# One piece split in each of eight epochs from the first sample on, with the second half's pieces first

## What is computed

```python
pooled = jnp.mean(x, axis=(2, 3))              # x is the normalized input here
att = jax.nn.sigmoid(pooled @ att_w.T + att_b)
agg_w = jnp.einsum('nk,kocij->nocij', att, weight)
out = conv_general_dilated(xi[None], wi, (1, 1), padding=[(1, 1), (1, 1)])   # per sample
x = x + conv(gn(x), weight, att_w, att_b)
```

## Time and profile before

| | |
|---|---|
| median of 3 runs | 1337.74 us (1337.7 to 1338.12) |
| the profiled execution | 1337.87 us |
| its span in the profile | 1335.7 us |
| TensorE (PE) busy | 1287.5 us, 96% |
| VectorE (DVE) busy | 1209.1 us, 91% |
| ScalarE (ACT) busy | 916.6 us, 69% |
| group matmuls, L480 | 6912, 1160.2 us |
| fp32 mix matmuls, L433 | 440, 74.7 us |
| fp16 mix matmuls, L442 | 1140, 87.1 us |

### The profile page before, as it was taken

How to read it: one execution, slowest core, us unless ns; L and a number is a source line. 1 busy time by engine, 2 the same in 40 slices (tenths; PEclk the granted TensorE clock), 3 DMA queues, 4 the chain that set the end, 5 groups by cost and what they waited for, 6 DMA issues and landing times.

```text
span 1335.7 us, 22954 instructions
## 1 busy us (share of the span) xinstructions
PE 1287.5 (96%) x8596; PEld 731.8 (55%) x8596; DVE 1209.1 (91%) x2121; ACT 916.6 (69%) x1441; POOL 56.8 (4%) x72
## 2 busy tenths in 40 slices
PE   1899999999999999999999999999999999999998
PEld 0455555555555555555555555555555555555555
DVE  7988999999999999999999998999989999998983
ACT  4875767867667676676867767677776767667531
POOL 0000000000000000000000000000000000000000
PEclk9899999999999999999999999999999999999999
DMA  9214644446543555534455452555525255552434
GB/s 381 99 22 125 180 115 104 129 130 176 143 107 108 137 157 145 144 89 133 141 145 156 98 145 77 149 139 145 145 54 153 84 146 145 128 154 60 98 98 142
DMA packets 30475, 174.59 MB, mean 131 GB/s; under 512 B 3488, under 2 KB 3744, under 8 KB 28320
## 3 DMA queue, kind: packets, MB, share of 16 engines
q1 hardware_dynamic: 20288, 113.94, 23.1%
q0 software_dynamic: 8928, 49.78, 22.2%
q10 hardware_dynamic: 1152, 9.44, 2.2%
HBM read 112.33 MB, written 51.38 MB: 123 GB/s over the span
## 4 chain that ended last, share of the span: by engine, by line
PE 95%; issue 4%; DVE 1%; POOL 0%; POOLq 0%; DVEq 0%
PE pM L480 86%; PE pG L442 4%; PE pG L433 4%; PE pS L415 0%; DVE Us L655 0%; DVE E L642 0%; POOL small L1321 0%; DVE Vs L660 0%; DVE T L636 0%; POOL sel L1317 0%; DVE X L767 0%; DVE small L901 0%; DVE small L890 0%; DVE small L889 0%; DVE small L891 0%
## 5 line engine op out<-in xcount | busy, mean ns | idle before, releaser
L480 PE MATMUL pM<-Vs,Us 128*128 128x385 f16 (+1 forms) x6912 | 1160.2, 330 | 2.6 <-DVE Us L655 2.6
L480 PEld LDWEIGHTS pM<-Vs,Us 128*128 128x128 f16 x6912 | 673.5, 98 | 495.7 <-issue 23.2
L1026 ACT CAST Vs<-E 128x784 f16<-128x784 f32 x192 | 159.8, 840 | 137.3 <-DVE E L628 72.2
L603 DVE SCALAR_TENSOR_TENSOR T<-X 128x392 f32<-128x392 f32 x384 | 193.4, 560 | 12.2 <-ACT X L1081 10.5
L660 DVE TENSOR_TENSOR Vs<-E,Vs 128x784 f16<-128x784 f32 x192 | 182.9, 969 | 4.0 <-ACT Vs L1026 4.0
L628 DVE SCALAR_TENSOR_TENSOR E<-T 128x784 f32<-128x784 f32 x128 | 119.1, 972 | 2.2
L1041 ACT ACTIVATE Us<-E 128x768 f16<-128x768 f32 x120 | 95.9, 835 | 35.6 <-DVE E L642 35.6
L642 DVE SCALAR_TENSOR_TENSOR E<-G,T 128x768 f32<-128x768 f32 x128 | 117.0, 955 | 2.2
L1101 ACT ACTIVATE unused<-X,small 128x784 bf16<-128x784 f32 x120 | 113.8, 949 | 3.9
L1062 ACT ACTIVATE X<-pM,small 128x392 f32<-128x392 f32 x128 | 74.6, 583 | 59.3 <-PE pM L480 59.2
L655 DVE SCALAR_TENSOR_TENSOR Us<-E,Us 128x768 f16<-128x768 f32 x120 | 111.8, 952 | 0.1
(11 more groups left out here) (83 smaller groups left out, 646.9 us busy)
## 6 DMA issues: line engine op xcount, KB each, us to landing
X<-x_dram SPq DMA_DIRECT2D x66, 784.0 KB, 5.4
out_dram<-X SPq DMA_DIRECT2D x64, 784.0 KB, 3.8
X<-x_dram POOLq DMA_DIRECT2D x62, 784.0 KB, 8.1
W<-w_dram SPq DMA_DIRECT2D x8, 1152.0 KB, 19.7
G<-W ACTq DMA_DIRECT2D x8, 1152.0 KB, 5.6
attw<-attw_dram SPq DMA_DIRECT2D x1, 128.0 KB, 8.3
small<-attb_dram SPq DMA_DIRECT2D x1, 0.5 KB, 8.9
```

The lines of the kernel that those rows point to most:

```text
L480: mm = pe.matmul(tile_rows(bank(k, o))[:, :, first:last], Us[:, j, a, c, o, kx, :], v_in(j, b, c, kx), start=(at < 2 and i == 0), stop=(i ...
L603: ins = dve.scalar_tensor_tensor(out=dst[c], in0=a[c], scalar=scale, in1=d[c], op0=ALU.mult, op1=ALU.add)
L1026: act.copy(v_out(j, 0), e_buf(n, ("V", chunk, j))).then_inc(v_hi, 1)
```

## The change

`SPLIT` now splits pieces 4, 5, 6, 7, 0, 1, 2, 3 in epochs 0 to 7, where epochs 1 to 8 split 0, 4, 1, 5, 2, 6, 3, 7. The mix waits for low parts in `mix_tile`, at tile 0 if a new piece is of half 0 and at tile 4 for all. In `epoch`, `w_low` comes before `v_low(n, 1, 4)`, `attention` and `add_rows(n, b, 3, 1)`. In the first epoch TensorE has logits and mix units earlier, and the lists of VectorE and ScalarE and their tables are in another order, with the split of piece 4 in them.

```diff
-SPLIT = ((), (0,), (4,), (1,), (5,), (2,), (6,), (3,), (7,))
+SPLIT = ((4,), (5,), (6,), (7,), (0,), (1,), (2,), (3,))
...
 U_LO_FIRST = [
-    (0, 2), (0, 1), (1, 2), (1, 1), (0, 3), (1, 3), (0, 0), (0, 4),
-    (1, 0), (1, 4), (1, 5), (0, 5),
+    (0, 1), (0, 2), (1, 1), (1, 2), (0, 3), (1, 3), (1, 0), (1, 4),
+    (0, 0), (0, 5), (0, 4), (1, 5),
 ]
...
             def mix_tile(n, m):
                 if not is_first(n) or m >= MIX_BANKS:
                     pe.wait_ge(taps_taken, n * TAKES + m - MIX_BANKS + 1)
+                if not is_first(n) and m in (0, FULL):
+
+                    new = [i for i in split_in(n - 1) if m == FULL or i < JT]
+                    if new:
+                        pe.wait_ge(w_lo, len(split_before(n - 1)) + len(new))
...
                 if u == 0:
                     pe.wait_ge(att_ready, n + 1)
-                    if split_in(n - 1):
-                        pe.wait_ge(w_lo, len(split_before(n)))
...
             group(0, 5, 0)
+            logits_mm(1)
             group(0, 5, 1)
             group(0, 6, 0)
-            logits_mm(1)
             group(0, 6, 1)
+            mix(1, 0)
             group(0, 7, 0)
             group(0, 7, 1)
             group(0, 8, 0)
-            mix(1, 0)
+            mix(1, 1)
             group(0, 8, 1)
-            mix(1, 1)
...
                 v_low(n, 1, 0)
                 add_rows(n, b, 3, 0)
+                if len(split_in(n)) > 0:
+                    w_low(n, 0)
                 v_low(n, 1, 4)
                 if more:
                     attention(n + 1)
                 add_rows(n, b, 3, 1)
-                if len(split_in(n)) > 0:
-                    w_low(n, 0)
```

More of the change, by code:

```diff
@@ L78 @@
 V_LO_FIRST = [
[L79 to L80 removed]
+    (0, 3), (0, 4), (0, 0), (0, 1), (0, 2), (1, 1), (0, 5), (1, 2),
+    (1, 0), (1, 3), (1, 5), (1, 4),
 ]
@@ L922, in _ @@
             norm_too(0, 0, 1, 1)
+            w_max(1)
             norm_too(0, 0, 1, 0)
-            v_pair(0, 0, 0, 3)
             dve.wait_ge(pool_step, K + 1)
             attention(0)
-            v_pair(0, 0, 0, 1)
+            w_max(0)
+            v_pair(0, 0, 0, 3)
+            v_single(0, 0, 0, 0)
             v_low(0, 0, 3)
             v_low(0, 0, 4)
-            w_max(1)
-            v_single(0, 0, 0, 5)
-            w_max(0)
+            v_pair(0, 0, 0, 1)
+            v_low(0, 0, 0)
+            u_pair(0, 0, 1)
             v_low(0, 0, 1)
-            u_pair(0, 0, 1)
             w_bound()
@@ L937, in _ @@
             w_scale()
-            v_low(0, 0, 5)
             unscales()
             u_pair(0, 1, 1)
+            u_low(0, 0, 1)
             u_low(0, 0, 2)
-            u_low(0, 0, 1)
+            u_low(0, 1, 1)
             u_low(0, 1, 2)
-            u_low(0, 1, 1)
             u_pair(0, 0, 3)
@@ L948, in _ @@
             u_low(0, 1, 3)
-            v_single(0, 0, 0, 0)
+            u_low(0, 1, 0)
+            v_single(0, 0, 0, 5)
+            u_low(0, 1, 4)
             u_low(0, 0, 0)
+            u_low(0, 0, 5)
             u_low(0, 0, 4)
             v_pair(0, 0, 1, 1)
-            v_low(0, 0, 0)
-            u_low(0, 1, 0)
+            v_single(0, 0, 1, 5)
+            v_low(0, 1, 1)
+            u_low(0, 1, 5)
             take_other(0, 2, 0)
-            u_low(0, 1, 4)
-            u_low(0, 1, 5)
-            u_low(0, 0, 5)
+            channel_stats(1)
+            take_other(0, 3, 0)
+            group_shift(1)
+            take_other(0, 2, 1)
+            group_variance(1)
+            take_edge(0, 0, 4, 0)
+            v_low(0, 0, 5)
+            norm_scale(1)
+            take_other(0, 3, 1)
+            take_edge(0, 0, 4, 1)
             v_pair(0, 0, 1, 3)
-            v_low(0, 1, 1)
-            take_other(0, 3, 0)
-            take_other(0, 2, 1)
+            v_low(0, 1, 2)
             v_single(0, 0, 1, 0)
[L964 to L970, removed]
+            w_low(0, 0)
+            attention(1)
+            v_low(0, 1, 0)
+            take_edge(0, 0, 5, 0)
             v_low(0, 1, 3)
-            take_edge(0, 0, 4, 1)
-            norm_scale(1)
-            take_edge(0, 0, 5, 0)
             take_edge(0, 0, 5, 1)
             add_rows(0, 0, 3, 0)
+            add_rows(0, 0, 3, 1)
             v_low(0, 1, 5)
             v_low(0, 1, 4)
-            attention(1)
-            v_low(0, 1, 0)
-            add_rows(0, 0, 3, 1)
             v_pair(1, 1, 0, 1)
             v_pair(1, 1, 0, 3)
+            take_other(0, 8, 0)
             v_low(1, 0, 1)
@@ L986, in _ @@
             v_low(1, 0, 2)
-            take_other(0, 8, 0)
             u_pair(1, 0, 1)
             take_other(0, 9, 0)
+            add_rows(0, 0, 9, 0)
+            take_other(0, 8, 1)
+            take_other(0, 9, 1)
+            v_low(1, 0, 4)
             u_low(1, 0, 1)
-            add_rows(0, 0, 9, 0)
-            v_low(1, 0, 4)
-            take_other(0, 8, 1)
+            u_pair(1, 1, 1)
+            take_edge(0, 0, 10, 0)
             u_low(1, 0, 2)
-            u_pair(1, 1, 1)
             u_pair(1, 1, 3)
-            take_other(0, 9, 1)
             u_low(1, 1, 1)
-            take_edge(0, 0, 10, 0)
             take_edge(0, 0, 10, 1)
@@ L1235, in _ @@
             take_taps(0, 8)
-            u_high(0, 0, 0)
+            sums(1, 1, 0, 0)
             u_high(0, 0, 1)
             u_high(0, 0, 2)
-            u_high(0, 0, 5)
+            u_high(0, 1, 1)
             u_high(0, 1, 2)
-            u_high(0, 1, 1)
+            sums(1, 1, 0, 1)
             u_high(0, 1, 0)
-            sums(1, 1, 0, 0)
+            u_high(0, 0, 0)
             u_high(0, 0, 3)
             u_high(0, 1, 3)
-            u_high(0, 0, 4)
[L1247 to L1251, removed]
+            u_high(0, 0, 5)
+            sums(1, 1, 1, 0)
+            u_high(0, 1, 4)
+            take_first(0, 0, 1)
+            take_first(0, 0, 0)
+            u_high(0, 0, 4)
+            u_high(0, 1, 5)
             take_first(0, 1, 0)
-            u_high(0, 1, 5)
-            v_high(0, 1, 1)
             take_first(0, 1, 1)
             take_pair(0, 0, 2, 0)
-            sums(1, 1, 1, 0)
+            v_high(0, 1, 1)
+            sums(1, 1, 1, 1)
+            w_aside_too(0)
             take_pair(0, 0, 2, 1)
+            take_pair(0, 0, 3, 0)
+            v_high(0, 0, 5)
+            take_pair(0, 0, 3, 1)
+            root(1)
             v_high(0, 1, 2)
-            take_pair(0, 0, 3, 0)
-            sums(1, 1, 1, 1)
-            take_pair(0, 0, 3, 1)
+            w_high(0, 0)
+            norm(1, 1, 1, 1)
+            exponential(1)
+            norm(1, 1, 0, 1)
+            norm(1, 1, 0, 0)
             v_high(0, 1, 3)
-            v_high(0, 1, 4)
-            root(1)
+            v_high(0, 1, 0)
+            take_taps(1, 0)
             v_high(0, 1, 5)
-            exponential(1)
             take_first(0, 6, 0)
[L1269 to L1272, removed]
             take_first(0, 6, 1)
-            norm(1, 1, 1, 1)
-            v_high(1, 0, 1)
-            take_taps(1, 0)
             take_taps(1, 1)
```

51 lines of the change are left out of this document (27 added, 24 removed), and 6 rows, old and new, of the table E_FIRST.

## The result

The changed kernel takes 1327.59 us (median of 4 runs, 1327.29 to 1328.99), the kernel before, run beside it, 1337.88. The ratio is 0.9923, with a 95% interval of 0.9909 to 0.9937: 10.3 us faster, where 11.0 were forecast (1326.8). The profiled execution is the slowest of the four, 1328.99 with a span of 1326.8; the other three have spans of 1325.1 to 1325.4.

A forecast was written before the change was run, and what follows sets the result against it. TensorE was taken as the bound, through matmul time and its pauses. −8.1 (pauses) − 4.8 (mix) + 1.9 (start) = −11.0 us against 1337.87 gave 1326.8, range 1323.3 to 1331.0.

The forecast's parts named there:

- What bounds the kernel: Whole kernel: TensorE is 95% of the chain, so only less matmul time or fewer TensorE pauses can shorten it.
- Term 1: Ahead of mixes 2 to 9: early w_low cuts TensorE's pauses, mostly from 1.42 to 0.46 us; −8.1 us.
- Term 2: Mixes 4 to 8: tiles wait for their slowest quarter, so halves whole earlier make mix units shorter; −4.8 us.
- Term 3: First 60 us and epoch 0: reordered lists and a new split delay groups 0 and 1; +1.9 us.
- The clock rule: Before the first group: a long idle gap halves TensorE's clock, so longer idle speaks against the change; one slow stretch assumed.
- Rival 1: First epoch: the start costs nothing, the walk of ScalarE's list being 2 us off; 1324.9, chance 0.14.
- rival 2: First epoch: start costs 4 to 6 us, by a second slow stretch and a partly exposed sum; 1329.9, chance 0.16.
- Rival 3: Mixes 1 to 8: each split piece pays by itself, 1.9 us gained instead of 4.8; 1329.7, chance 0.03.
- Rival 4: Ahead of the mixes: the pause is not the wait for w_lo and stays; 1334.9, chance 0.04.
- rival 5: Epoch 0: ScalarE becomes the bound, its four sums delaying groups 0 to 3; slower, 1341.2, chance 0.03.
- The range: Whole kernel: 1323.3 to 1331.0, from the start's two bounds and half a microsecond for the pauses.

The follow-up runs named there:

- order of the pieces: Kernel before with only SPLIT changed to (), 4, 5, 6, 7, 0, 1, 2, 3: 1335.37 us, ratio 0.9981.
- sums late: Changed kernel with piece 5's weight sum ahead of pieces 6 and 7's, and ScalarE's sums behind u_highs and takes groups 0 to 2 need: 1325.92 us.
- all: Changed kernel with piece 5's weight sum first, sums behind the u_highs, and w_low and attention ahead of add_rows(3,0) and v_low(1,4): 1324.33 us.
- piece 5's sum first: Changed kernel with piece 5's weight sum ahead of pieces 6 and 7's on ScalarE, and w_bound and scales earlier on VectorE: 1325.94 us.
- both early: Changed kernel with w_low and attention ahead of add_rows(3,0) and v_low(1,4) behind the first epoch: 1324.16 us, ratio 0.9895.
- w_low alone: Kernel before with only w_low moved ahead of v_low(1,4), attention and add_rows(3,1) in epochs that split a piece: 1330.31 us, ratio 0.9943.
- the old start and both early: Changed kernel with the kernel before's first-epoch lists, SPLIT starting with (), and w_low and attention ahead of add_rows(3,0) and v_low(1,4): 1324.19 us.
- the extra clock matmuls: Changed kernel with 60 matmuls that compute nothing ahead of the first group, not 40: 1326.76 us.

## Why the prediction was right, point by point

**What bounds the kernel.** Right: all of the gain is on TensorE's path, while busy time on VectorE (1209.1 to 1208.0) and ScalarE (916.6 to 915.7) stayed.

**Term 1, the pauses, −8.1.** Right in mechanism and size. 0.46 was forecast for what remains of each pause; the stretches of 6.36 less 5.94 leave 0.42, and ahead of mix 8 0.16 against 0.22. The edit alone brought 7.7 us at the median and 7.9 in the profile behind mix 1. VectorE's lag was absorbed: TensorE waits only those six times between 170 and 1300 us.

**Term 2, the mix, −4.8.** Right. The order of the pieces alone brought 2.7 us of 2.9 expected (2.8 in the profile behind mix 1), and the unit times are those of the earlier trace rows.

The two together were 12.9 and measured 13.2 in the profile, from the end of mix 1 on.

**Term 3, the start, +1.9.** The mechanisms were named and the size was too small. The profiled execution lost 4.3 us, the median about 2.9 (13.2 less 10.3). Two numbers in it failed. The first group was put at 53.8 and started at 54.52, since the last piece's load let ScalarE go on at 37.1 and not at 36.4; in other executions of the same lists it started at 53.1. That the mean of the four is the forecast 53.8 is partly luck, since the prediction took landings as fixed. And the wait at group 1 was put at 0.6 us, because I laid the slow stretch of the kernel before into group 0 again. There it would have hidden 1.65 us of that wait. In the profile of the change it came behind, so that both showed: 2.31 us of wait and 1.65 of slow clock. Group 1's distance from group 0, 8.2 us in my walk and 8.45 measured, was right as a number and not in its cause: the walk had ScalarE's second sums() set it, and with the sums moved back it stayed at 8.44, set by VectorE's list. As forecast, TensorE waited neither at groups 2 and 3 nor ahead of mix 1. The total came within 0.8 us because terms 1 and 2 gained 0.3 more and the start cost 1.0 more than forecast.

**The clock rule.** I quoted the Trainium skill, TensorE: Matmul & The Clock Gate, "Why this matters for your kernels", on long idle gaps, as speaking against this change. The traces agree that half clock follows idle time: behind the first group's start every slow stretch began during a gap of 2.2 to 3.8 us of TensorE or within 1.5 us of its end. But gaps of 2.2 and 2.3 us were followed by one in some profiles (sums late, all) and gaps of 2.0 to 2.4 us in others not (piece 5's sum first, order of the pieces), and the longer gaps of 3.37 and 3.67 us ahead of the first group (changed, both early) were followed by none until the next gap, at group 1. So here a longer gap meant neither a longer stretch nor a surer one. The second rival's second slow stretch did not come in any profile: behind the first group's start none has more than one.

**The rivals.** Rival 1 (start for nothing) and 2 (4 to 6 us) bracket what was seen: the profiled execution by itself, with 4.3 us, is in rival 2's range, the median between it and the forecast. Rival 2's mechanism did not come, though: no second slow stretch, and no wait at group 2 or 3. Rivals 3 and 4 are refuted by the order alone and by w_low alone. Of rival 5, the sums ahead of the u_highs, next to nothing showed: in the changed kernel VectorE waits 0.51 us for the first u_high, and moving the sums back in the kernel with piece 5's sum first gave nothing, because VectorE's list ends at the same time.

**The range.** Two sums in it are slightly off. The bounds of term 3, −1 and +6, give 1324.0 and 1331.0 with the other terms, not 1323.8 and 1330.8, and half a microsecond more makes the upper end 1331.5, not 1331.0.

**What the prediction did not follow up.** It said that the wait at tile 4 adds nothing here and would count only if attention came early, and both were right. It did not go on to ask what an early attention would bring. With both ahead of the work that nobody waits for, the pauses go altogether, for 3.4 us more: 1324.16 us is the fastest version measured, level with the old start and both early (1324.19), which leaves the first epoch alone.

**Open.** Whether the extra clock matmuls help, what decides where the slow stretch falls in a given execution, and why the edits of the start gain 1.6 us in the changed kernel and nothing at the median in the one with both early. That a shorter list of VectorE ahead of group 1 would remove its 2.3 us was not tried.

## What to carry to other kernels

When TensorE waits for two things that one engine makes in turn, look at what stands ahead of the later one and can wait longer: here two pieces of VectorE's work swapped places for 7.7 us, and two more moved back for another 3. Where matmuls run side by side in quarters of the array, convert whole sets first, since here a set with one slow member was as slow as before. And a slow stretch of the clock can hide a wait: price a wait at full clock, and count the slow stretch apart.

## What was not expected of the hardware

The slow stretch behind the start is not fixed to the kernel. In twelve profiles, TensorE's granted clock of 0.50 behind the first group's start lasted 3.4 us when it came: in six of them it began within 1.5 us of the first group's start, in three 8 to 9 us behind it, and in three it did not come. With the new lists it costs 1.65 us or nothing. The landing of the last weight piece moves the same start by another 1.4 us. Executions of one kernel with new lists lie 0.6 to 2.2 us apart, those with the old ones 0.4 to 1.2. That these two causes make up that spread is likely but not shown, since only one execution of each kernel has a trace.

A piece of VectorE's work of 2.61 us moves everything behind it by 2.53 (183.17 to 185.70): neighbours overlap by about 0.08 us. The prediction had taken it from the rows before (2.52 us). On a list of some 130 operations an epoch such terms add up.
